# One fused transformer front on one core: the prologue of a patch-token kernel written out call by call, with patch statistics on ScalarE

## The reference

```python
# x (32, 3, 96, 96), txt (32, 77, 256)
h = tok(x)                        # 16x16 patches -> layernorm(768) -> @ Wp + bp -> layernorm(256)
h = concatenate([h, txt], axis=1) # 32 sequences of 36 + 77 = 113 tokens, width 256
h = h + attn(layernorm(h))        # 16 rotary heads of 16, RMS-normed q and k, causal,
                                  # differential: softmax_0 - lam * softmax_1, 8 value heads of 32
h = h + ffn(layernorm(h))         # fp4_linear gate and up (704), silu(gate) * up, fp4_linear down
# fp4_linear: input and weight are both rounded to FP4 (E2M1), in blocks of 16 with a scale each
```

## Time and profile before

| | |
|---|---|
| three timed runs | 549.67, 550.25, 553.76 us; median 550.25 us |
| the profiled execution | 553.06 us, of which the span from the first to the last instruction is 551.3 us |
| mean granted TensorE clock | 0.969 of full speed |
| busy: PE, DVE, ACT, POOL | 495.3, 488.3, 311.4, 267.3 us |

### The profile page before, as it was taken

How to read it: one execution, slowest core, us unless ns; L and a number is a source line. 1 busy time by engine, 2 the same in 40 slices (tenths; PEclk the granted TensorE clock), 3 DMA queues, 4 the chain that set the end, 5 groups by cost and what they waited for, 6 DMA issues and landing times.

```text
span 551.3 us, 13752 instructions
## 1 busy us (share of the span) xinstructions
PE 495.3 (90%) x3628; PEld 405.4 (74%) x3628; DVE 488.3 (89%) x1317; ACT 311.4 (56%) x709; POOL 267.3 (48%) x357
## 2 busy tenths in 40 slices
PE   5676666899999999999999978899999999999985
PEld 4564544677777777777777666799888888888974
DVE  5898976788999999999999798989999999999972
ACT  2234223677777777777777866845455544444421
POOL 3354444545444445554444534655555555555540
PEclk9989878899999999999999998999999999999998
DMA  8830001011111111111111120022111121121111
GB/s 196 302 114 27 18 20 32 24 31 49 52 51 51 51 51 51 51 51 51 49 46 55 43 64 27 28 67 57 50 55 57 57 57 57 57 57 51 45 40 42
DMA packets 34156, 32.13 MB, mean 58 GB/s; under 512 B 6130, under 2 KB 32466, under 8 KB 34130
## 3 DMA queue, kind: packets, MB, share of 16 engines
q1 hardware_dynamic: 34130, 31.82, 19.9%
HBM read 23.09 MB, written 8.71 MB: 58 GB/s over the span
## 4 chain that ended last, share of the span: by engine, by line
PE 74%; DVE 16%; issue 4%; ACT 3%; DMA 1%; POOL 0%; SPq 0%; DVEq 0%; ACTq 0%; POOLq 0%
PE bank L153 31%; PE bank_a L153 16%; PE bank L821 5%; PE bank L833 5%; PE bank L812 4%; PE bank L1466 3%; PE bank L846 2%; PE bank_b L862 2%; PE bank_a L777 2%; DVE st L440 1%; DMA wp_raw<-in_wp 1%; PE bank_b L1474 1%; DVE wf L487 1%; PE bank_a L781 1%; PE bank_b L667 1%
## 5 line engine op out<-in xcount | busy, mean ns | idle before, releaser
L907 ACT ACTIVATE pt<-bank 113x452 f32<-113x452 f32 x128 | 60.2, 553 | 42.9 <-PE bank L821 42.9
L1321 POOL TENSOR_TENSOR h_deq<-fh,fhb 128x704 f32<-128x704 f32 x29 | 40.3, 1391 | 68.1 <-DVE fhb L1192 65.6
L153 PE MATMUL bank<-wgu_hi,fx_hi 128*128 128x512 f32 x174 | 66.4, 382 | 2.3 <-DVE fx_lo L1245 2.3
L153 PE MATMUL bank<-wgu_hi,fx_lo 128*128 128x512 f32 x174 | 66.0, 379 | 0.0
L153 PE MATMUL bank<-wgu_lo,fx_hi 128*128 128x512 f32 x174 | 65.9, 379 | 0.0
L977 POOL TENSOR_TENSOR rope<-rope,trig 113x256 f32<-113x256 f32 x64 | 49.2, 788 | 22.8 <-DVE rope L1015 22.8
L984 POOL TENSOR_TENSOR rope<-rope 113x512 f32<-113x512 f32 x32 | 41.0, 1282 | 31.4 <-DVE rope L1021 30.9
L153 PE MATMUL bank_a<-wd_hi,fh_hi 128*128 128x256 f32 x174 | 53.6, 308 | 2.3 <-DVE res L1199 2.3
L153 PE MATMUL bank<-wqkv_hi,xo_hi 128*113 128x512 f32 (+1 forms) x128 | 48.0, 375 | 4.7 <-DVE rope L1015 3.4
L153 PE MATMUL bank_a<-wd_lo,fh_hi 128*128 128x256 f32 x174 | 50.6, 291 | 0.0
L153 PE MATMUL bank_a<-wd_hi,fh_lo 128*128 128x256 f32 x174 | 50.6, 291 | 0.0
(11 more groups left out here) (179 smaller groups left out, 1499.1 us busy)
## 6 DMA issues: line engine op xcount, KB each, us to landing
xb<-h_dram SPq DMA_DIRECT2D x29, 129.0 KB, 2.1
rb<-h_dram SPq DMA_DIRECT2D x29, 128.0 KB, 2.1
h_dram<-h SPq DMA_DIRECT2D x32, 112.9 KB
out<-res SPq DMA_DIRECT2D x28, 128.0 KB, 1.7
px<-in_patches SPq DMA_DIRECT2D x9, 384.0 KB, 8.7
hx<-in_txt SPq DMA_DIRECT2D x32, 77.0 KB
hr<-in_txt SPq DMA_DIRECT2D x32, 77.0 KB
wf<-in_wgu SPq DMA_DIRECT2D x1, 1408.0 KB, 7.4
```

Source lines behind the costliest of these rows:

```text
L153: last = pe.matmul(dst, a(k), w(k), start=(start and n == 0), stop=(n == len(passes) - 1))
L907: act.activation(pt[0:T, r, :, :].rearrange("p s t -> p (s t)"), sc_ps[r][0:T, :], ACT.Exp, scale=1.0 / math.sqrt(HD)).then_inc(m["exp_mad ...
L1321: pool.tensor_tensor(blocks(h_deq[:, 0:INTER], BLK), blocks(h_code[:], BLK), spread(h_scale[:], BLK), ALU.mult).then_inc(f["h_deq"], 1)
```

## The change

All of it lies ahead of the loop, but for one wait.

1. The function `steps` of the front is gone on every engine, and the attention steps ahead of the loop are no longer called by `steps`. Instead five functions (`tensor_prologue`, `vector_prologue`, `scalar_prologue`, `gpsimd_prologue`, `sync_prologue`) list every call of the front and of the first attention steps in an order of their own. The loop, the transition and the feed-forward are as before.
2. `patch_sums` on DVE goes, and the aggregate in `variances` with it. ACT takes `patch_mean` (a Copy with an accumulated output, 128x768) and `patch_square` (a Square with an accumulated output, 128x768) for each of the 9 tiles.
3. The gain of `wp` is six ACT activations of 128x256 in place of one DVE instruction of 128x1536; the matmuls of the average wait for each of the six apart. The centring on DVE is cut in two.
4. The scales and inverses of the weight blocks are taken in three batches of pieces, not in eight; the maxima stay one per piece.
5. Inputs: `cols` (gains, biases and the rotary table, one array), `bias_rows` (three rows, one array, spread over the partitions) and `lambdas` (one array) take the place of ten. `wp` comes in two halves. The attention weights are loaded ahead of the feed-forward weights, and `wgu` behind patch tile 4.
6. All weight transposes use one bank (`bank_b`), which is also that of the transposes of q and k, so that `masks(0)` no longer waits for them; the feed-forward's first product waits for the last `w_low`. `h2` is used as the source of zeros.
7. The split of the attention weights into high parts is cut in two, and that of the projection is apart.

```diff
-            def patch_sums(i):
-                dve.wait_ge(px_loaded[i], 16)
-                for n in range(2):
-                    dve.bn_stats(st1[:, 6 * n:6 * n + 6], px[:, i, n * PD // 2:(n + 1) * PD // 2]).then_inc(k["patch_stats"], 1)
...
             def variances(i):
 
-                if i + 1 < PT:
-                    dve.wait_ge(k["patch_stats"], 3 * (i + 1) + 2)
-                    dve.bn_aggr(means[i % 2][:, 0, :], st1[:]).then_inc(k["patch_stats"], 1)
                 if i >= 0:
...
+            def w_scales(i):
+
+
+                b = batch_blocks(i)
+                dve.wait_ge(k["w_amax"], BATCHES[i][-1] + 1)
...
+            def w_inverse(i):
+                b = batch_blocks(i)
+                dve.wait_ge(k["w_short"], i + 1)
                 dve.reciprocal(winv[:, b], wshort[:, b]).then_inc(k["w_inv"], 1)
...
+            def gain_weights(c):
+
+                act.wait_ge(k["columns_loaded"], 16)
+                act.wait_ge(wp_loaded[2 * c // KP], 16)
+                act.activation(wp_sb[:, c, :], wp_raw[:, c, :], ACT.Copy, scale=columns[:, c:c + 1]).then_inc(k["wp_gained"], 1)
...
+            def patch_mean(i):
+
+                act.wait_ge(px_loaded[i], 16)
+                after(act, k["patch_stats"], 2 * i)
+                act.activation(px_used[:], px[:, i, :], ACT.Copy, scale=-PD ** -1.5,
+                               accum_out=px_shift[:]).then_inc(k["patch_stats"], 1)
+
+            def patch_square(i):
+                act.wait_ge(k["patch_stats"], 2 * i + 1)
+                after(act, k["variances"], i - 1)
+                act.activation(px_used[:], px[:, i, :], ACT.Square, bias=px_shift[:], scale=PD ** -0.5,
+                               accum_out=means[(i - 1) % 2][:, 0, 1:2]).then_inc(k["patch_stats"], 1)
...
             def masks(s, odd):
 
-                if isinstance(s, int) and s == 0:
-                    pe.wait_ge(k["w_low"], len(groups))
-                    pe.wait_ge(k["token_biased"], PT)
-                    pe.wait_ge(k["patch_copied"], 2 * PT)
...
-            for i in range(-1, PT - 5):
-                front(i)
-            for b in range(FIRST, LOOP[0]):
-                if b < 2:
-                    front(PT - 1 + b)
-                steps(b, b % 2)
+            prologue(engine, front, stages)
             with engine.Fori(LOOP[0], LOOP[1] - 1, step=2) as b:
```

```diff
+            pe.wait_ge(k["token_biased"], 7); p.project(7); pe.wait_ge(k["patch_copied"], 17)
+            pe.wait_ge(k["patch_copied"], 18); pe.wait_ge(k["token_biased"], 8); a.masks(0, 0); a.scores(0, 0)
+            a.qk_transposes(1, 1); a.qk(3, 1); a.pv(0, 0); pe.wait_ge(m["exp_made"], 3); p.project(8)
...
+            pe.wait_ge(k["w_low"], 6); p.w_transposes(6); a.scores(5, 1); pe.wait_ge(k["w_low"], 7)
+            p.w_transposes(7); a.qk(7, 1); pe.wait_ge(k["w_low"], 8); p.w_transposes(8); pe.wait_ge(k["w_low"], 9)
```

456 lines of the change are left out of this document (269 added, 187 removed).

## The result

The changed kernel takes 536.52 us in the median of 4 runs (534.79 to 536.88); the kernel before, beside it on the same chip, 552.0 us (549.67 to 554.98, 4 runs). The ratio is 0.971, with a 95% interval of 0.965 to 0.977: faster by 2.9%. The forecast was 532.6 us with a range of 522 to 546. The profiled executions are 553.06 and 536.75 us, 16.3 apart where the forecast took 17.6. The front brought more than forecast; part of it was lost again behind the front.

The account below looks back on a forecast made before the run. DVE was taken to bound the front: 15.2 start + 48.9 + 54.9 ends DVE at 119.0, v(6) at 118.2 instead of 135.8, gain 17.6; 550.25 - 17.6 = 532.6 us, range 522 to 546.

Parts of the forecast that it names:

- The bound and its point in time: Front up to the loop: DVE ends last, at 119.0, and PE starts v(6) at 118.2 instead of 135.8.
- the sum's term for the front: Front ahead of the loop: v(6) on PE starts 17.6 us earlier, 135.8 - 118.2.
- DVE's work: DVE ahead of its loop: work falls by 15.0 us, from 112.3 to 97.3 us.
- The density: DVE's busy share in the front: 94% for the first 46 us of work, 88% for the second 48.3 us.
- the nearest row is 110 to 135.8, with 88%: Second half of DVE's front, attention with weight pieces between: 48.3 us of work at 88% takes 54.9 us.
- The start: DVE's centring of `wp`, its first long piece: 0.7 us earlier, at 15.2 instead of 15.94, bounds 0 and 2.
- 0.86 us an activation: ACT's 18 activations of 128x768 in the front: 15.5 us, up to 19, hidden behind DVE's 97.
- The rival in which these squares hold up the chains: Front's second half: ACT's and PE's queues keep DVE at 72%; gain 5.4 us, 545 us; chance 0.20.
- What the removed work was worth: DVE's front: patch statistics save 9.1 us and their aggregates 1.7, within 15.0 us less work together.
- Blocking by POOL: DVE's front: some 8 us of busy time lost to POOL stays as before; bounds 3 and 14.
- The clock rival: PE ahead of the loop: short pauses keep its clock low, v(6) at 159, 573 us, slower; chance 0.04.
- the span behind v(6) unchanged at 415.5: Everything from v(6) on: same code, so 551.3 - 135.8 = 415.5 us stays; wrong if it moves over 2 us.

Follow-up runs that it names:

- with the door moved: Changed kernel with PE's wait for the last w_low moved from ahead of the loop to before the q and k transposes inside it: 532.67 us, ratio 0.9632.
- the 8 clears: Changed kernel with eight more one-column memsets at the start of DVE's program: 533.2 us, one run.
- 4 clears: Changed kernel with four more one-column memsets at the start of DVE's program: 529.55 us, one run.

## Why the prediction was right

**The bound and its point in time.** Right: the front was what could be gained, and DVE sets its end. v(6) starts 0.44 us after DVE's last `w_low` ends (114.41), 2.16 us after PE had come to the door. v(6) was forecast at 118.2 and came at 114.85; the sum's term for the front was 17.6, measured 20.97.

**DVE's work.** Forecast 97.3 us up to its loop, measured 95.24. (The parts of the forecast's saving add up to 14.8, not to the 15.0 that it took.) Its last piece ahead of the loop, the `var<-moments` that starts at 114.85, ends at 115.00, where the forecast had 119.0.

**The density.** The mis-sized term, in both halves. Taken were 94% for the first and 88% for the second, from windows of the old order. Measured were

```profile
15.20:65.00 49.80, 42.14 (x210) 33.63 (x208) 45.24 (x121) 33.53 (x89) 26.25 (x31) 0.97 0.33 110
65.00:114.30 49.30, 42.72 (x372) 30.54 (x372) 46.94 (x126) 35.28 (x92) 28.61 (x37) 1.00 0.11 33
```

91% and 95%: the step that fell short is "the nearest row is 110 to 135.8, with 88%" for attention with weight pieces between. That row was a stretch in which PE was already full (25.61 of 25.8 us), so it was no measure of what DVE can do. From the centring at 16.04 to the end at 115.00 DVE is busy 92.85 of 98.96 us, 93.8%, where the forecast's two halves together make 90.8%. Of the 4.0 us by which DVE ends earlier than forecast, this gives 3.3 and the smaller work 1.6; the later start takes 0.8 back. Of the 4.6 us in which DVE is idle in the first of these windows, 0.8 lie ahead of the centring and 1.9 ahead of the first two token tiles, behind PE.

**The start.** DVE's first long piece was forecast at 15.2 and began at 16.04, later than before. The rows:

```profile
7.74 5.46 PE L652 MATMUL bank_b<-wp_raw,b_wide 128*128 128x256 f32 x12 [2.15 <-issue]
12.99 3.01 PE L660 MATMUL bank_a<-wp_sb,average 128*128 128x256 f32 x12
```

The halves of `wp` did land early. But PE has two groups of 12 passes ahead of the centring, and the first takes 5.46 us and the second 3.01, since PE is at half clock until 13.5 us in this execution (12.6 in that of the kernel before, whose groups took 5.01 and 2.75). Fewer column loads could not help there. Where the clock came up at 12.2 us, with statistics on DVE, the centring began at 15.42, and at 11.6, with the door moved, at 15.09. So the forecast's 15.2 was within what an execution may give; the 0.8 us is the chance of this one.

**ACT.** Forecast 0.86 us an activation, with 0.2 more as the upper bound for the accumulator. The groups of the kernel after up to 115 us:

```profile
L544 ACT ACTIVATE px_used<-px,px_shift 128x768 bf16<-128x768 f32 x9 | 8.4, 931 | 0.1
L538 ACT ACTIVATE px_used<-px 128x768 bf16<-128x768 f32 x9 | 7.6, 840 | 2.0 <-DMA px<-in_patches 1.9
L525 ACT ACTIVATE wp_sb<-wp_raw,columns 128x256 f32<-128x256 f32 x6 | 2.6, 495 | 0.3 <-DMA wp_raw<-in_wp 0.3
L538 ACT ACTIVATION_READ_ACCUMULATOR px_used<-px 128x1 f32 x9 | 1.8, 195 | 0.0
L544 ACT ACTIVATION_READ_ACCUMULATOR px_used<-px,px_shift 128x1 f32 x9 | 1.7, 191 | 0.0
```

19.5 us in all, where 15.5 was taken and 19 was the bound. ACT comes to 76.43 us, within the 74.6 to 78. It hid, as forecast. The rival in which these squares hold up the chains lost here, but the kernel with statistics on ACT in the old order shows its mechanism (6.9 us of DVE's waits): it was real, and the order decided.

**What the removed work was worth.** The sum divides DVE's work by a density, and so counts every us off DVE as at least a us of time, 10.8 for the statistics. Over the whole front the sum came out near, since the work was right and the density 3 points too low. For this part alone the price does not hold: putting the statistics back costs 4.8 us in the new order, 5.2 at v(6), since DVE runs denser with them and its other rows get shorter. A density is not a constant of the engine that stays when work is taken away.

**Blocking by POOL.** "The sum keeps the 8 of before": right. Taking for each line and shape of DVE's single rows up to the loop the time above its fastest instance gives 9.4 us before and 10.4 after. It only moved to other lines. L399, the successor of the 525 ns in the earlier trace rows, has 277 ns now; L404, which writes `y`, has 584 where its fastest took 390. One instance, in the timelines of POOL and DVE:

```profile
48.78 1.97 POOL L952 TENSOR_TENSOR rope<-rope,columns 113x256 f32<-113x256 f32 x2 [1.89 <-DVE rope L990]
49.34 0.83 DVE L404 TENSOR_SCALAR y<-y,means,t 128x256 f32<-128x256 f32 x1
```

From the rule of the Trainium skill ("SBUF — State Buffer", section "Who interferes with whom"), that a DVE instruction with two SBUF inputs contends with a GpSimd instruction that reads SBUF, the forecast had expected more of it in a shorter front. The total is 1.0 us above the one before, so the trace agrees in sign; the 2 or 3 us that the forecast gave it were not reached.

**The clock rival.** It did not come true in the front (0.97 and 1.00). It did come true for 1.4 us at one place which the forecast had not looked at: the pause at the door. The Trainium skill's warning about pauses between bursts ("TensorE: Matmul & The Clock Gate", section "HAM oscillation — how this bites in real kernels") bears on it. At the door this case shows one pause of 2.16 us with one fall behind it. In the tail it shows falls one after the other: the clock reads 0.50 from 516 to 518.5 us, 1.00 from 519 to 521.5, 0.50 from 522.5 to 525, 1.00 from 526 to 528.5 and 0.50 from 529 to 532, with PE busy 0.88 of 2.5 and 0.45 of 2.5 us in the two stretches between.

**The step that failed: "the span behind v(6) unchanged at 415.5".** It is 535.0 - 114.85 = 420.15, 4.65 us more, over the 2 us that the forecast set itself as its limit. The anchors part it, as the lead on the kernel before: 20.97 at v(6); 19.48 at masks(6), so 1.5 at the door, by the clock; 19.04 at the masks of sequence 31 (7.08 us per sequence against 7.06); 19.76 at feed-forward tile 3, which gives 0.7 back at the transition; 18.02 at tile 21, so 1.74 by the period of 7.19 us; 16.27 at the last tile, 1.75 in the tail. For the first and the fourth of these there are experiments. The tail's loss goes with them. From the fourth-last tile to the last, starts of `res`, it is 17.54 us in the kernel after and 15.69 in the kernel before, and over the fourteen profiles 17.2 to 17.5 in the five with DVE's program of the kernel after and 15.6 to 16.2 in the nine others: the 8 clears bring it to 15.99. A tile there takes 5.0 us where the clock stays up and 6.2 to 6.6 where it falls; the kernel after has two tiles of the longer kind in a row (6.53 and 6.58), the kernel before one (6.22, then 5.04). Why one tile more is of that kind with the longer period, no run shows. The clock's rise at the start is no part of these 4.65 us, which are counted from v(6) on. "Everything behind that point is the same code" was true, and the conclusion from it was not: the same code met another clock, and another place in the program.

## What to carry to other kernels

Taking work off the busiest engine helps only if the engine that gets it has it done before it is asked: the same 18 activations were worth +4.8 us in an order made for them and -5.2 in one that was not. A density measured where another engine is the bound says nothing of what an engine can reach alone. Where a prologue hands over to a loop, let each wait stand in front of the first instruction that needs it, since a pause of 2 us on PE can cost its own length and the half clock behind it. And two single profiles that differ by 1 us at some point may differ only in when the clock came up: compare the spans between two fixed points, not the points.

## What the hardware did that was not expected

- DVE's loop costs 0.1 us more in each feed-forward tile at one place in its program than at others: 7.19 against 7.10 us, 0.47 against 0.37 us across the jump back, bound to the DVE program in all fourteen profiles, and removed by eight tiny memsets, or four, in front. The same five profiles lose another 1.0 to 1.9 us in the last three tiles, where PE's clock falls in one tile more.
- An accumulated output on ACT stands in the trace as an instruction of its own, 0.19 us each, which starts shortly before the activation's recorded end (22.86 + 0.93 and 23.70 above), 3.5 us for 18.
- PE starts at half clock, 0.43 us from pass to pass of 256 columns, and comes up to 0.22 us at a moment that differs between executions, 10.5 to 14.2 us. The first group of 12 passes took 5.46 us in the kernel after and 4.30 with 4 clears, with the same code on PE, and the windows, which read 1.00 there, do not show it.
- PE's clock fell behind a pause of 2.15 or 2.16 us in five of six executions, for 1.0 to 1.5 us of loss, and stayed up in the sixth.
